# A graph network: a third of layer 2's tiles by gathered table rows, the counts turned in layer 1, and a ruler moved to SBUF

## What is computed

```python
for l in range(2):
    W = einsum('rb,bdf->rdf', w_coe[l], bases[l])
    T = einsum('nd,rdf->rnf', h, W)
    msg = T[etype, src] * norm
    h = segment_sum(msg, dst, N) + h @ self_loop[l]
    h = relu(gamma[l] * (h - mean[l]) * rsqrt(var[l] + eps) + beta[l])
```

## Time and profile before

| | us |
|---|---|
| median of 3 runs (lowest, highest) | 5907.89 (5897.45, 5912.18) |
| the profiled execution, its time | 5911.12 |
| its span in the profile | 5909.4 |
| first and last leftover gather of layer 2 | 2798.2, 4073.8 |
| mean granted TensorE clock | 0.855 |

### The profile page before, as it was taken

One profiled execution on the slowest core, in us unless ns is written; L12 is line 12 of the kernel. 1 busy time (PEld: TensorE's weight loads), 2 busy tenths in 40 slices (PEclk: granted clock), 3 DMA queues, 4 the chain that ended last, 5 costly groups with the idle time before them and its releaser, 6 DMA issues. The chain is left out here.

```text
span 5909.4 us, 157242 instructions
## 1 busy us (share of the span) xinstructions
PE 4289.3 (73%) x54120; PEld 3252.4 (55%) x54121; DVE 4190.3 (71%) x9549; ACT 1869.0 (32%) x2646; POOL 2482.1 (42%) x2045
## 2 busy tenths in 40 slices
PE   5666667666666666664999999997983666666697
PEld 2345445544445445443666666665442666666687
DVE  4377777777777777776777777776116999999823
ACT  2111111111111111111666666664001555555500
POOL 0477666666666666661000000000000777777400
PEclk9788788787787788786999999998996888888899
DMA  5444444444444444444777777775963344444388
GB/s 199 163 136 129 128 129 123 120 127 127 128 130 127 128 129 119 125 127 128 244 243 246 246 244 246 243 247 183 303 218 111 120 152 152 152 152 152 117 282 253
DMA packets 701393, 1008.83 MB, mean 171 GB/s; under 512 B 147635, under 2 KB 607774, under 8 KB 688126
## 3 DMA queue, kind: packets, MB, share of 16 engines
q1 hardware_dynamic: 618290, 779.49, 41.3%
q0 software_dynamic: 56448, 115.72, 7.8%
q10 hardware_dynamic: 26572, 112.71, 4.9%
HBM read 728.15 MB, written 279.47 MB: 171 GB/s over the span
## 5 line engine op out<-in xcount | busy, mean ns | idle before, releaser
L619 POOL DMA_INDIRECT f_rows<-table,f_recs x1715 | 1685.4, 983 | 924.2 <-issue 623.6
L710 PE MATMUL f_acc<-f_rows,f_hot 128*128 128x264 f32 x3430 | 1133.3, 492 | 739.4 <-DVE f_rows L946 710.3
L710 PEld LDWEIGHTS f_acc<-f_rows,f_hot 128*128 128x128 f32 x3430 | 812.1, 246 | 949.1 <-issue 479.3
L2004 PE MATMUL a_psum<-state_and_spare,a_weights 128*128 (+1 forms) x4802 | 654.5, 306 | 304.6 <-DVE a_weights L2122 164.4
L1954 POOL TENSOR_TENSOR a_weights<-a_powers,a_counts 128x896 f32<-128x896 f16 x245 | 718.1, 2936 | 343.8 <-ACT a_powers L2044 317.5
L2004 PEld LDWEIGHTS a_psum<-state_and_spare,a_weights 128*128 128x128 f32 x4802 | 644.1, 222 | 318.0 <-issue 215.4
L1194 ACT ACTIVATE g_grow<-g_gps 128x1024 f16<-128x1024 f32 (+1 forms) x637 | 629.8, 989 | 442.6 <-PE g_gps L1126 442.6
L1142 PE MATMUL g_zps<-g_ohot,g_grow 32*128 32x256 f16 x19992 | 661.3, 269 | 14.5 <-ACT g_grow L1194 14.5
L1109 POOL DMA_INDIRECT g_grow<-high_low_rows,g_lcur x49 | 61.1, 1246 | 1330.0 <-PE g_zps L1142 1215.7
L1142 PEld LDWEIGHTS g_zps<-g_ohot,g_grow 32*128 32x128 f16 x19992 | 459.7, 93 | 176.5 <-issue 124.4
L1238 DVE TENSOR_SCALAR g_ohot<-count,slot_target 128x256 f16<-128x256 f16 x2499 | 530.7, 281 | 0.2 <-PE g_zps L1142 0.2
(11 more groups left out here) (273 smaller groups left out, 5921.8 us busy)
## 6 DMA issues: line engine op xcount, KB each, us to landing
f_rows<-in_edge_attr SPq DMA_DIRECT2D x343, 320.0 KB, 3.2
g_srow<-slot_sources SPq DMA_DIRECT2D x245, 320.0 KB, 4.8
counts_by_source_f<-state_and_spare ACTq DMA_DIRECT2D x49, 1568.0 KB, 7.1
state_and_spare<-counts_by_source_f SPq DMA_DIRECT2D x343, 224.0 KB, 3.7
counts_by_destination_f<-state_and_spare SPq DMA_DIRECT2D x343, 224.0 KB, 2.4
no_edge_penalty<-g_pen SPq DMA_DIRECT2D x343, 224.0 KB, 2.7
s_ring<-counts_by_destination_f SPq DMA_DIRECT2D x98, 784.0 KB, 4.3
a_pen<-no_edge_penalty SPq DMA_DIRECT2D x49, 1568.0 KB, 10.1
```

The costliest lines, as they stand in the source:

```text
L619: e.indirect_dma_start(out=rows[:, j, 0:D], out_offset=None, in_=k.table_d[0], in_offset=bass.IndirectOffsetOnAxis(ap=recs[:, j, 4:5].bitc ...
L710: m = e.matmul(acc[:, 0:GW], hot[:, j, :], rows[:, j, :], start=j == 0, stop=j == SLOTS - 1)
L2004: m = e.matmul(psum[:, 4 + i // 3, i % 3 * (D + 4):i % 3 * (D + 4) + D + 1], weights[:, j, i * P:(i + 1) * P], k.msg[:, bass.ds(hb * SEG + ...
```

## The change

Layer 1 gets work that layer 2 had or needs. `table_rows` multiplies each finished tile by the 8 weights of layer 2, and ScalarE stores the table. `turn_counts` moves here: TensorE transposes counts into one PSUM bank, `flipped`, and ScalarE (`move_turned`) copies it twice, as counts and as penalty (Relu(1e34 - count x 1e34)), and issues both stores. The counts by source are stored block by block. The bank for `flipped` is the ruler's: `count_up` is now read from the SBUF tensor `count16`. The penalty changes sign and its user subtracts it.

Layer 2 does two of three tiles by products as before. The third is done by gathers from the table, half of its 36 slots beside each product tile: GpSimd's `messages` (3 groups of 6), VectorE's `send`, TensorE's `sum_messages` after batches 2, 6 and 10, and `close_half`. The last tile is a product tile alone: 33 product tiles and 16 gathered. The two PSUM banks of gathered rows are handed over one by one (`PAIRS`), with a copy of 512 columns each. The engines' loops have bodies of one product tile, VectorE's and SyncE's of two.

```diff
+UNIT = 3
+UNITS = NT // UNIT
+HALF_GROUPS, HALF_PER = 3, 6
+HALF_SLOTS = HALF_GROUPS * HALF_PER
...
-FAR = -3.0e38
+FAR = -1.0e34
...
-        count_up = cells(pb("count_up", [P, 512])[:, :], False)
-        eighths = count_up.rearrange("p (j e) -> p j e", e=RELATIONS)[:, :, 0]
+        count_up = k.count16[:, 0:P]
+        eighths = k.count16[:, :].rearrange("p (j e) -> p j e", e=RELATIONS)[:, :, 0]
+        flipped = pb("flipped", [P, 512])[:, :].bitcast(F16)[:, 0:SW]
...
+        FLIP_AT = {3: 0, 4: 1, 5: 2, 6: 3}
+        FLIP_LATER = {0: 4, 1: 5, 2: 6}
...
-                e.wait_ge(t_sb, t)
+                e.wait_ge(table_sb, t * 2)
...
+            def turn_counts(t, g):
+                e.wait_ge(cnt_moved, t * (len(BLOCKS) * QUARTERS) + blocks_of(g) * QUARTERS)
+                e.wait_ge(by_dst_moved, t * NSEG + g)
+                for i in range(SEG):
+                    m = e.transpose(flipped[:, i * P:(i + 1) * P], mine[:, g * SEG + i, :], k.ident16[:, :])
+                m.then_inc(turned, 1)
...
+            def table_rows(t, half):
+                if half:
+                    e.wait_ge(table_sb, t * 2 + 1)
+                else:
+                    e.wait_ge(t_sb, t + 1)
+                e.matmul(pm[:, :], ht[:, :], k.wr[:, 1, half * (TW // 2):(half + 1) * (TW // 2)], start=True, stop=True)\
+                 .then_inc(table_ps, 1)
...
+                        if g in (3, 4):
+                            table_rows(t - 1, g - 3)
                         if 2 <= g < 2 + len(BLOCKS):
                             count(t - 1, g - 2)
-            tile(0, True)
-            with e.Fori(1, NT) as t:
-                tile(t, False)
+                        if g in FLIP_AT:
+                            turn_counts(t - 1, FLIP_AT[g])
+                        elif not second:
+                            turn_counts(t - 2, FLIP_LATER[g])
...
+            def move_turned(t, g):
+                w = g % FLIP_SLOTS
+                e.wait_ge(turned, t * NSEG + (g + 1))
+                e.wait_ge(by_dst_out[w], (t * slot_uses(g) + g // FLIP_SLOTS) * 32)
+                e.activation(by_dst[:, w, :], flipped, ACT.Copy)
+                e.activation(pen[:, w, :], flipped, ACT.Relu, bias=far[:, 0:1], scale=FAR)
+                e.drain().then_inc(by_dst_moved, 1)
+                e.wait_ge(by_dst_moved, t * NSEG + (g + 1))
+                for to, row in ((k.cd_d[False], by_dst), (k.pen_d, pen)):
+                    e.dma_start(to[bass.ds(t, 1), :, g * SW:(g + 1) * SW].rearrange("a p c -> (a p) c"), row[:, w, :])\
+                     .then_inc(by_dst_out[w], 16)
...
+                move_turned(t, len(BLOCKS) - 1)
...
+        SUM_AT = {2: 0, 6: 1, 10: 2}
...
+                def records(n, i, v, g):
+                    c = e.value_load(k.tlo[0:1, bass.ds(i * UNIT + 2, 1)], min_val=0, max_val=REAL_CHUNKS)
+                    e.wait_ge(ring, n * HALF_GROUPS + (g + 1))
+                    at = (v * HALF_SLOTS + g * HALF_PER) * REC
+                    e.dma_start(recs[:, g * HALF_PER:(g + 1) * HALF_PER, :].rearrange("p a b -> p (a b)"),
+                                k.rec_d[bass.ds(c * (CHUNK * REC), P * 2 * HALF_SLOTS * REC)]
+                                .rearrange("(p c) -> p c", p=P)[:, at:at + HALF_PER * REC]).then_inc(rec_in[g], 16)
...
+                def unit(i, final):
+                    for v in range(2):
+                        for p in range(SPIECES):
+                            e.wait_ge(s_made, i * (2 * SPIECES) + (v * SPIECES + p + 1))
+                            piece(i * UNIT + (1, UNIT)[v], p)
+                            if p % 2 == 1 or p == SPIECES - 1:
+                                if v == 0:
+                                    records(i * 2 + 1, i, 1, p // 2)
+                                elif not final:
+                                    records(i * 2 + 2, i + 1, 0, p // 2)
...
+                def messages(n, g):
+                    e.wait_ge(rec_in[g], (n + 1) * 16)
+                    e.wait_ge(ring, n * HALF_GROUPS + (g + 1))
+                    e.sem_inc(turn, 1)
+                    for j in range(g * HALF_PER, (g + 1) * HALF_PER):
+                        e.indirect_dma_start(
+                            out=rows[:, j, :], out_offset=None, in_=k.table_d[1],
+                            in_offset=bass.IndirectOffsetOnAxis(ap=recs[:, j, 4:5].bitcast(I32), axis=0),
+                        ).then_inc(gathered[g], 16)
+                e.wait_ge(hl_out, 16)
+                with e.Fori(0, 2 * UNITS) as n:
+                    messages(n, 0)
+                    leftover(n)
+                    messages(n, 1)
+                    messages(n, 2)
+                leftover(2 * UNITS)
...
+                def gather(n, t, h):
+                    lo, hi = PAIRS[h]
+                    e.wait_ge(s_made, n * SPIECES + ((hi - 1) // SPIECE + 1))
+                    e.wait_ge(g_sb, n * NPAIR + (h + 1 - GBANKS if h >= GBANKS else 0))
+                    for c in range(lo, hi):
...
+                def sum_messages(n, g):
+                    e.wait_ge(gathered[g], (n + 1) * (16 * HALF_PER))
+                    e.wait_ge(hot_made, n * HALF_GROUPS + (g + 1))
+                    if g == 0:
+                        e.wait_ge(acc_free, n)
+                    for j in range(g * HALF_PER, (g + 1) * HALF_PER):
+                        m = e.matmul(acc[:, 0:D], hot[:, j, :], rows[:, j, :], start=j == 0, stop=j == HALF_SLOTS - 1)
+                    m.then_inc(ring, 1)
+                def tile(n, t, final):
                     for b in range(1, NB):
-                        gather(t, b)
-                        scatter(t, b - 1)
-                        if b in TURN_AT:
-                            turn_counts(t, TURN_AT[b])
-                    scatter(t, LASTB)
-                    if not final:
-                        gather(t + 1, 0)
-                    turn_counts(t, LAST_TURN)
-                    transform(t)
+                        for h in pairs(b):
+                            gather(n, t, h)
+                        for h in pairs(b - 1):
+                            scatter(n, h)
+                        if not final and b in SUM_AT:
+                            sum_messages(n, SUM_AT[b])
...
-                        e.wait_ge(g_ps, t * NB + (b + 1))
                         e.wait_ge(scattered, t * NB + (b - (GSLOTS - 1) + 1 if GSLOTS - 1 <= b < LASTB else 0))
-                        n = len([c for c in BATCHES[b] if c != LEFT])
-                        e.activation(grow[:, gslot(b), 0:n, :], gps[:, :, :].rearrange("p a (i f) -> p (a i) f", i=2)[:, 0:n, :],
-                                     ACT.Copy).then_inc(g_sb, 1)
-                        if TURN_AT.get(b) in BY_ACT:
-                            g = TURN_AT[b]
-                            e.wait_ge(turned, t * NSEG + (g + 1))
-                            e.wait_ge(stored[g], t * 32)
-                            e.activation(cdr[:, g, :], tps, ACT.Copy).then_inc(cd_act, 1)
+                        for h in pairs(b):
+                            e.wait_ge(g_ps, t * NPAIR + (h + 1))
+                            e.activation(grow[:, gslot(b), PAIRS[h][0] % BATCH:(PAIRS[h][1] - 1) % BATCH + 1, :],
+                                         gps[:, h % GBANKS, :].rearrange("p (i f) -> p i f", i=2), ACT.Copy).then_inc(g_sb, 1)
...
-                def move_counts(t, g):
-                    e.wait_ge(stored[g], t * 32)
-                    if g in BY_DVE:
-                        e.wait_ge(turned, t * NSEG + (g + 1))
-                        e.tensor_copy(cdr[:, g, :], tps)
-                        e.drain().then_inc(cd_dve, 1)
-                    else:
-                        wait_moved(e, t, g)
-                    e.tensor_scalar(pen[:, g, :], cdr[:, g, :], 0.0, FAR, ALU.is_equal, ALU.mult).then_inc(pen_made, 1)
...
+                def send(n, i, g):
+                    q = slice(g * HALF_PER, (g + 1) * HALF_PER)
+                    e.wait_ge(rec_in[g], (n + 1) * 16)
+                    e.wait_ge(ring, n * HALF_GROUPS + (g + 1))
+                    e.tensor_scalar(near[:, q], recs[:, q, 0], k.tbase[:, bass.ds(i * UNIT + 2, 1)], None, ALU.add)
+                    e.drain()
+                    e.tensor_tensor(hot[:, q, :], repeat(k.count16[:, 0:P], HALF_PER), spread(near[:, q], P), ALU.is_equal)\
+                     .then_inc(hot_made, 1)
...
+                def close_half(n, i, v):
+                    t = i * UNIT + 2
+                    e.wait_ge(ring, n * HALF_GROUPS + 2 * HALF_GROUPS)
+                    e.scalar_tensor_tensor(hm[:, :], acc[:, 0:D], k.norm[:, bass.ds(t, 1)],
+                                           hm[:, :] if v else k.self_[:, bass.ds(t, 1), :].rearrange("p a f -> p (a f)"),
+                                           ALU.mult, ALU.add)
+                    e.drain().then_inc(acc_free, 1)
+                    if v:
+                        close(t, hm[:, :])
...
```

(27 more changed lines are left out.)

247 lines of the change are left out of this document (128 added, 119 removed).

## The result

The changed kernel takes 5814.39 us (median of four executions, 5807.34 to 5825.42), the kernel before 5910.03 in the same comparison: a ratio of 0.9843, with an interval from 0.9821 to 0.9865. It is faster by 96 us, where 188 were forecast. The time lies in the range of the prediction and the direction is right; half of the gain is missing.

The account below looks back on a forecast made before the run. VectorE and TensorE's loop bounds layer 1 (51.2 us a tile; GpSimd takes over at 55.3), TensorE bounds layer 2. 5911.1 + 197 + 17 - 400 = 5725 us profiled, 5722 as median; own range 5640 to 5800, 8 in 10 5560 to 5870.

Parts of the forecast that it names:

- the hold: Layer 1: gathers beginning under VectorE instructions with two SBUF operands wait for their end, 11.2 us a tile, bounds 0 to 14.
- the 1.27 among its signs: Layer 1, expected in the profile: gathers of line 619's kind with a mean near 1.27 us instead of 0.98.
- Rival 1: Layer 1: the ruler in SBUF costs GpSimd nothing, gathers stay at 0.944 us; 5590 us, chance 0.20.
- so VectorE is not slower for it: Layer 1, ruler moved to SBUF: VectorE's instructions keep their length, as lines 856, 858 and 859 take 1.49, 1.49, 1.48 us.
- The loop of VectorE and TensorE: Layer 1, with tables and transposes added: 51.2 to 54 us a tile, still under GpSimd's 55.3.
- rival 3: Layer 1: TensorE waits for ScalarE's release of the flips' single PSUM bank; 5974 us at 60.5 us a tile, chance 0.13.
- The tail: End of layer 1: ten flips of 2.6 us one after another, about 40 us instead of 23, +17 us.
- Layer 2: 33 product tiles instead of 49, at 27.3 us each, 31 of them plus a last of 22.2: minus 400 us.
- hold each other: Layer 2: GpSimd's and TensorE's loops, both near 26.7 us, leave each other no slack, so 27.3 us a tile.
- 0.05 us a gather: Layer 2: what a gather loses under line 1238's 0.22 us instructions (line 1338 after), 0.9 us a tile in all.
- Rival 2: Layer 2: every gather pays 0.31 us, 29.6 us a tile, +71; 5796 us, chance 0.15.
- same operands, same width: After layer 2: the penalty's sign change keeps VectorE's instruction and is put at nothing.

Follow-up runs that it names:

- run 3: The changed kernel with every eighth number of the ruler (`eighths`) packed into its own SBUF tensor: 5655.43 us, ratio 0.9567 to the kernel before.
- run 1: The kernel before with only the whole ruler of layer 1 read from SBUF: 6228.75 us, against 5913.51 for the kernel before on the same chip.
- run 2: The kernel before with the plain ruler read from SBUF and `eighths` left in PSUM: 5912.8 us, tile 51.26 us.
- run 4: The changed kernel with the ruler back in PSUM and the flips in bank `pm`, with added waits: 5631.49 us, ratio 0.9532 to the kernel before.
- run 8: The kernel before with the two operands of the attention's maximum exchanged (line 2079, 2197 after): 5920.98 us beside 5914.27.

## Why the prediction came out as it did

**Which engine bounds layer 1: right.** GpSimd passes VectorE and TensorE, its waits for records go, and the hold is near the size that was worked out. The prediction added 11.2 us to the 34.4 us of gathers, which have 0.98 us each and so hold what lines 858 and 859 cost already. Packed (run 3), 35 x (1.257 - 0.984) = 9.6 us came, with 1.0 us more of gaps (35 x 0.305 against 9.7), and the tile is 54.6 us where it had 55.3. (Its sum makes a mean of 45.6/35 = 1.30 us; the 1.27 among its signs counts from 0.944 and does not fit it.) The nearness is luck in part. Put down to the VectorE instruction under which each gather begins, 600 to 2600 us of run 3, line 927's kind costs 4.0 us a tile (forecast 5.0), those of lines 842, 805 and 916 cost 2.0, 1.9 and 1.3 (1.65, 1.56, 1.13), and the seven of line 945, forecast at 1.9, next to nothing: one gather a tile begins under any of them and loses 0.05 us. Rival 1 (the ruler costs GpSimd nothing) falls with runs 1 and 2.

**The step that failed: "so VectorE is not slower for it".** It was read from lines 856, 858 and 859, which step through the ruler one number at a time, and was applied to lines 842 and 805 with "2040, 1960 ... columns, so at that rate 2.27, 2.18". Those two read every eighth number, 16 bytes apart. Measured in SBUF: 3.84 and 3.62 us. The hold grows with the instruction: 35 x (1.347 - 0.984) = 12.7 us a tile on top of the kernel before, where 9.6 came in run 3 and 11.2 were forecast. Between run 3 and the changed kernel, which differ in this alone, lie 3.17 us a tile and 159 us in all; the gathers that begin under the two instructions lose 6.5 us a tile in the changed kernel and 3.9 in run 3. With `eighths` packed the forecast of 5722 would have met 5655, an error of the other sign. The Trainium skill, "Advanced Engine Details and Errata", Memory Cachelines, has the rule that was not weighed: SBUF has lines of 16 bytes, wants two accesses in each for full speed, and is slower where each access goes to another line. The trace agrees, with 1.88 ns a column against 1.12 for the same numbers packed in SBUF. In PSUM the same step shows no such loss: 2285 ns there (run 4) and 2286 packed (run 3).

**The loop of VectorE and TensorE: at the end of its range.** "51.2 to 54" is 54.0 by run 4, with that run's own waits. The prediction asked only whether it stays under GpSimd's 55.3, and it does. But the bound underneath decides what the repair is worth: from 57.75 about 3.7 us a tile are to be had, not the 6.6 that were lost. Part of the 54.0 is TensorE at half clock (two sums of 4.7 us in run 4's tile), and 1.5 and 2.1 us come back with more transposes.

**The flips (rival 3): hidden.** TensorE does wait for ScalarE's release of the bank, 95.7 us in 2000 us, 2.8 us a tile, but beside GpSimd's longer tile, which is 57.59 us without any flips (run 1). Where VectorE and TensorE are the bound they are not free: there tables, flips and the added waits together are the 2.8 us between 51.2 and 54.0. ScalarE has room for them: 22.1 us a tile busy (765.6/34.6) besides its issues; the prediction's terms for both add up to 29 us, not to its 31. The DMAs fit: 177 GB/s at a share of 0.58, on 126 at 0.44.

**The tail: +21.5 us, forecast +17.**

**Layer 2: right in kind, a little low in worth, -431 for -400.** A tile is 26.3 us ((3990.2 - 3149.4)/32), forecast 27.3; 32 x 1.0 is the 31 us. TensorE was put at 26.8 and is the bound at 26.3, at a granted clock of 1.00 as forecast. What was wrong is GpSimd: 26.6 was forecast and 19 x (0.996 + 0.30) = 24.6 measured. It then waits for the last scatter (27.5 us in 19 tiles, 1.4 us each), so there is slack, and the 0.6 us that were added on top of 26.7 for two loops that "hold each other" did not come. The message gathers have a mean of 0.996 us, not 1.1:

```profile
L1198 POOL DMA_INDIRECT g_rows<-table,g_recs x342 | 341.3, 998 | 104.3 <-issue 103.3 <-DVE g_lcur L1384 0.9
...
L1338 DVE TENSOR_SCALAR g_ohot<-count,slot_target 128x256 f16<-128x256 f16 x973 | 215.6, 302 | 40.8 <-PE g_zps L1243 36.4 <-issue 2.7
```

So line 1338, one input from SBUF, busy for 11.3 us of each tile, costs hardly anything; the price of 0.05 us a gather from its like was too high. It does hold: the message gathers that it makes longer end 0.82 us after it, as with line 1229. But a gather takes 0.94 us anyway, so what is left of an instruction costs only beyond 0.12 us, and the prediction counted all of it. Put down to the instruction under which each of the 576 message gathers begins, line 1338 costs 0.2 us a tile where 0.9 were forecast, line 1329 costs 0.3 (0.7), and the one-hots of line 1349 cost 0.4 (1.3, with the closings). Rival 2 (each gather pays 0.31 us) falls.

**The rest: -15.7 us, forecast 0.** Of these 8.6 are the instruction of run 8, which the prediction put at nothing for "same operands, same width"; its length hangs on GpSimd's product beside it. The other 7 were not followed, and may be scatter: the same piece is 1805 to 1820 us in the four profiles of the kernel before and its variants, and 1787 to 1803 in the ten of the changed kernel and its variants.

The errors partly cancel: +119 in layer 1, +10 at its two ends, -31 in layer 2, -16 in the rest, 82 in all, which is 5725 against the 5807 of the profiled execution.

## What to carry to other kernels

Before an operand changes memory, look at its step in each use: a rate read from a neighbour with step 1 says nothing of one with a step of 16 bytes, and a packed copy of 104 bytes a partition was worth 159 us here. A VectorE instruction with two SBUF inputs is also paid for by GpSimd's transfers that it holds, so put its length, not only its own delay, into the sum; what counts of it is what is left when the transfer begins, less 0.12 us here. And where TensorE waits often, measure the clock before cutting its work: filling its waits with transposes that nobody needs made the best kernel of this study, 5526.51 us in one execution, 5568.13 timed with two rounds, 0.9419 of the kernel before.
